# 31 of 135 products of ones taken out of a fused attention and expert layer

## The reference

```
q   = ln(x) * g + b                     # self-attention: 16 heads of width 8
x   = x + mha(q, q)                     # 512 x 512 scores per head
qc  = ln(x) * g + b ;  kv = ln(ctx) * g + b     # ctx: 154 tokens per sequence
x   = x + mha(qc, kv)                   # 512 x 154 scores per head
h   = ln(x) * g + b                     # eight experts, two chosen per token
out = x + sum over the 2 chosen e of gate_e * (gelu(h @ fc1_e.T + b1_e) @ fc2_e.T + b2_e)
```

## Time and profile before

| | |
|---|---|
| median of 3 runs | 272.69 us (272.57 to 273.06) |
| the profiled execution | 272.78 us |
| its span, first to last instruction | 270.8 us |
| TensorE busy | 248.6 us, 1699 matmuls |
| VectorE busy | 184.0 us |
| ScalarE busy | 162.2 us |
| GpSimd busy | 61.6 us |
| mean granted TensorE clock | 0.974 |

### The profile page before, as it was taken

How to read it: one execution, slowest core, us unless ns; L and a number is a source line. 1 busy time by engine, 2 the same in 40 slices (tenths; PEclk the granted TensorE clock), 3 DMA queues, 4 the chain that set the end, 5 groups by cost and what they waited for, 6 DMA issues and landing times.

```text
span 270.8 us, 5195 instructions
## 1 busy us (share of the span) xinstructions
PE 248.6 (92%) x1699; PEld 141.1 (52%) x1699; DVE 184.0 (68%) x369; ACT 162.2 (60%) x289; POOL 61.6 (23%) x110
## 2 busy tenths in 40 slices
PE   6899999999999999899999999998999999999540
PEld 2354533433333433345453455334699999999430
DVE  3859689999989889567554499764377455455543
ACT  3383465676776879869676413871576776766300
POOL 3560000000022020000222020175105700036372
PEclk9999999999999999999999999999999999999955
DMA  7107131240322220530110310013302261122232
GB/s 238 43 9 282 68 90 44 69 113 18 87 65 84 80 80 2 165 114 0 28 61 5 87 32 5 4 50 93 86 19 61 74 189 41 31 59 61 68 87 69
DMA packets 18634, 19.37 MB, mean 72 GB/s; under 512 B 2805, under 2 KB 15025, under 8 KB 18609
## 3 DMA queue, kind: packets, MB, share of 16 engines
q1 hardware_dynamic: 15089, 10.36, 13.2%
q10 hardware_dynamic: 2496, 6.59, 7.6%
q0 software_dynamic: 1024, 2.10, 2.7%
HBM read 9.13 MB, written 5.51 MB: 54 GB/s over the span
## 4 chain that ended last, share of the span: by engine, by line
PE 78%; DVE 9%; issue 3%; POOL 3%; ACT 2%; DMA 2%; POOLq 1%; DVEq 0%; ACTq 0%
PE ps_o L1108 11%; PE ps_r L1184 10%; PE ps_r L1175 10%; PE ps_r L1088 9%; PE ps_o L971 7%; PE ps_r L1046 6%; PE ps_x L946 3%; PE ps_r L982 3%; DVE row_max L808 2%; PE ps_o L1120 2%; PE ps_x L971 2%; PE ps_r L1058 2%; PE ps_o L1115 2%; PE ps_x L975 2%; ACT probs L654 2%
## 5 line engine op out<-in xcount | busy, mean ns | idle before, releaser
L654 ACT ACTIVATE probs<-ps_r 128x1024 f32<-128x1024 f32 (+1 forms) x88 | 83.6, 984 | 26.1 <-PE ps_r L1088 23.2
L804 DVE TENSOR_REDUCE row_max<-ps_r 128x2 f32<-128x1024 f32 x64 | 76.0, 1222 | 13.4 <-PE ps_r L1046 11.9
L704 ACT ACTIVATE parts<-ps_r,staged 128x128 f32<-128x128 f32 x120 | 33.2, 379 | 17.2 <-PE ps_r L1175 16.0
L1108 PE MATMUL ps_o<-probs,v_aug 128*9 128x512 f32 x256 | 33.3, 594 | 0.0
L541 POOL CAST max_part<-row_max 128x16 fp32r<-128x16 f32 x16 | 3.1, 196 | 128.9 <-issue 92.8
L971 PE MATMUL ps_o<-ones_bf 128*128 128x512 bf16 x114 | 32.4, 382 | 0.0
L1175 PE MATMUL ps_r<-rows_T,staged 128*128 128x128 f32 x240 | 30.8, 277 | 0.5 <-DVE staged L893 0.5
L1046 PE MATMUL ps_r<-k_tile,q_tile 32*128 32x512 f32 x128 | 29.9, 480 | 0.9 <-ACT probs L654 0.7
L1184 PE MATMUL ps_r<-staged,parts 128*128 128x128 f32 x240 | 30.7, 275 | 0.0
L1088 PE MATMUL ps_r<-q_tile,k_tile 32*128 32x512 f32 x128 | 29.3, 484 | 1.5 <-ACT probs L654 1.0
L808 DVE TENSOR_REDUCE row_max<-ps_r 128x4 f32<-128x616 f32 x32 | 24.3, 794 | 8.1 <-PE ps_r L1058 7.8
(11 more groups left out here) (161 smaller groups left out, 282.9 us busy)
## 6 DMA issues: line engine op xcount, KB each, us to landing
fc_sb<-fc_w ACTq DMA_DIRECT2D x8, 514.0 KB, 3.6
q_tile<-parts SPq DMA_DIRECT2D x36, 64.0 KB, 2.1
places_in<-o_raw ACTq DMA_DIRECT2D x2, 960.0 KB, 5.2
places_out<-rows_in SPq DMA_DIRECT2D x30, 64.0 KB
rows_in<-places_in SPq DMA_DIRECT2D x6, 256.0 KB, 3.4
k_tile<-parts SPq DMA_DIRECT2D x12, 64.0 KB, 2.1
x_sb<-x SPq DMA_DIRECT2D x2, 256.0 KB, 4.6
fc_sb<-w_rep SPq DMA_DIRECT2D x1, 512.0 KB, 5.3
```

What stands on the lines that cost most here:

```text
L654: nc.scalar.activation(probs[:, i:i + w], ps_r[:, slot("s", r), 0:w], ACT.Exp, scale=SCALE).then_inc(s_read, 1)
L704: ins = nc.scalar.activation(hidden[:, n % HIDDEN, c], ps_r[:, slot("s", r), 0, c * P:c * P + P], ACT.Gelu, bias=staged[:, o % STAGES, 2 * ...
L804: nc.vector.tensor_reduce(heads[:, 2 * pair:2 * pair + 2, t], ps_r[:, slot("m", r)], AX.X, ALU.max).then_inc(m_read, 1)
L1108: mm = nc.tensor.matmul(ps_o[32 * j:32 * j + DH + 1, :], v_aug[:, b, c, 4 * g + j], probs[:, region(n) + j], start=first, stop=last, tile_ ...
```

## The change

Where a word goes away altogether, its wait goes with it. The core of the diff, from the first and the last third of the list:

```
-    ... qk0:2 warm:1 max:1 warm:1 qkl:1 warm:5
-    qkl:2 ctx_hat:0 v:0 max:4 clear:3 zero:0 warm:5 max:3 ...
+    ... qk0:2 warm:1 max:1 qkl:1 warm:2 qkl:2
+    ctx_hat:0 v:0 max:4 clear:3 zero:0 warm:3 max:3 ...
...
-    max:82 neg:12 max:86 proj:2 warm:5 mT:12 ln:4 max:84 max:87
-    max:90 hat:4 warm:3 max:95 neg:13 warm:5 mT:13 max:88 max:91 warm:3 hT:4 max:89 warm:2 max:93 warm:2 router:0
+    max:82 neg:12 max:86 proj:2 warm:3 mT:12 ln:4 max:84 max:87
+    max:90 hat:4 warm:3 max:95 neg:13 warm:4 mT:13 max:88 max:91 warm:2 hT:4 max:89 warm:2 max:93 warm:2 router:0
...
-    oc:15 oT:15 warm:5 osT:3 warm:2 proj:3 warm:3 gT:0 ln:5 hat:5 warm:6 xT:0 warm:3 hT:5 fc1:0
+    oc:15 oT:15 warm:4 osT:3 proj:3 warm:2 gT:0 ln:5 hat:5 warm:1 xT:0 warm:3 hT:5 fc1:0
```

More of the change, by code:

```diff
@@ L69 @@
 ORDER_OF_STEPS = """
[L70 to L89, removed]
@@ L90 @@
-    pv:32 oc:8 scores:75 scores:67 neg:10 ln:3 oT:8 scores:74 hat:3 warm:1 pv:35 mT:10 pv:34 oc:9 hT:3 scores:73
-    warm:1 pv:39 q:3 scores:72 pv:38 oc:11 scores:71 oT:9 scores:70 pv:37 oT:11 pv:36 warm:2 max:80 oc:10 oT:10
-    max:83 max:81 warm:2 max:85 warm:1 osT:2 warm:1 max:82 neg:12 max:86 proj:2 warm:5 mT:12 ln:4 max:84 max:87
-    max:90 hat:4 warm:3 max:95 neg:13 warm:5 mT:13 max:88 max:91 warm:3 hT:4 max:89 warm:2 max:93 warm:2 router:0
-    scores:81 rank:0 scores:79 neg:14 warm:5 mT:14 scores:80 max:92 pv:43 max:94 neg:15 scores:77 prefix:0 scores:76
@@ L95 @@
[L95 to L108, removed]
+    ln:0 hat:0 ln:1 ctx_ln:0 hT:0 hat:1 clear:0-1 warm:4 qk0:0-1 clear:2 qk0:2 warm:1 max:1 qkl:1 warm:2 qkl:2
+    ctx_hat:0 v:0 max:4 clear:3 zero:0 warm:3 max:3 max:0 warm:1 max:5 warm:3 max:7 hT:1 qk0:3 max:2 warm:2 max:6
@@ new lines @@
+    v:1 neg:0 qkl:3 warm:3 mT:0 fill:0 warm:1 max:22 max:17 max:23 k:1 warm:5 scores:6 max:20 warm:1 scores:4 warm:3
+    max:19 warm:3 scores:1 max:21 ctx_T:0 max:16 warm:1 scores:7 warm:1 max:18 warm:3 scores:3 max:28 pv:3 max:24
+    scores:5 neg:2 warm:1 mT:2 max:25 max:31 max:8 q:1 scores:0 pv:2 scores:2 max:11 scores:19 warm:2 max:26 warm:1
+    ctx_vA:0 scores:23 max:30 pv:0 max:29 scores:20 max:27 warm:2 scores:18 max:15 pv:1 oc:0 neg:3 max:12 scores:17
+    mT:3 max:10 warm:1 pv:9 scores:22 load_fc:0 max:13 oT:0 scores:16 scores:21 max:14 pv:11 max:47 scores:30 max:9
@@ new lines @@
+    pv:10 scores:24 max:43 pv:8 max:42 scores:27 warm:2 max:53 neg:1 mT:1 oc:2 scores:31 max:54 ctx_k:0 scores:25
+    warm:2 max:45 scores:26 pv:15 max:49 scores:28 load_fc:1 max:44 pv:12 scores:29 max:48 warm:1 oT:2 scores:12
+    scores:14 max:41 max:46 warm:3 scores:13 max:40 warm:1 pv:13 scores:10 neg:5 max:51 pv:14 oc:3 max:55 kc_diag:0
+    scores:15 mT:5 max:32 warm:3 scores:9 load_fc:2 max:50 pv:6 scores:11 max:52 pv:7 max:36 scores:8 max:37 neg:6
+    pv:5 mT:6 scores:43 max:38 pv:4 oT:3 oc:1 scores:46 load_fc:3 scores:47 max:33 warm:1 oT:1 scores:40 warm:1
@@ new lines @@
+    max:35 scores:42 warm:1 osT:0 max:34 warm:1 scores:41 max:39 pv:21 neg:4 scores:44 load_fc:4 max:63 proj:0
+    scores:48-49 pv:23 ln:2 max:60 scores:45 pv:20 scores:51 hat:2 warm:1 scores:50 max:59 mT:4 pv:22 scores:52
+    max:58 hT:2 max:56 oc:5 max:61 scores:54 q:2 scores:53 pv:24 scores:32 scores:55 pv:25 max:62 scores:33
+    load_fc:5 pv:26 scores:38 max:57 pv:27 scores:34 max:67 max:66 neg:7 oc:6 scores:39 max:64 mT:7 pv:16 scores:35
+    max:68 scores:37 load_fc:6 oT:5 pv:19 scores:36 max:65 warm:1 max:70 pv:17 max:69 scores:58 ctx_vB:0 scores:56
@@ new lines @@
+    max:78 scores:61 pv:18 oT:6 oc:4 neg:8 scores:59 max:71 scores:60 oT:4 scores:57 max:76 pv:29 mT:8 max:79
+    scores:62-63 neg:9 pv:28 mT:9 max:77 max:74 neg:11 pv:30-31 oc:7 mT:11 max:72 scores:66 scores:65 load_fc:7
+    warm:2 oT:7 max:75 scores:64 pv:33 osT:1 max:73 scores:69 scores:68 proj:1 pv:32 oc:8 scores:75 scores:67 neg:10
+    ln:3 oT:8 scores:74 hat:3 warm:1 pv:35 mT:10 pv:34 oc:9 hT:3 scores:73 warm:1 pv:39 q:3 scores:72 pv:38 oc:11
+    scores:71 oT:9 scores:70 pv:37 oT:11 pv:36 warm:2 max:80 oc:10 oT:10 max:83 max:81 warm:2 max:85 warm:1 osT:2
@@ new lines @@
+    warm:1 max:82 neg:12 max:86 proj:2 warm:3 mT:12 ln:4 max:84 max:87 max:90 hat:4 warm:3 max:95 neg:13 warm:4
+    mT:13 max:88 max:91 warm:2 hT:4 max:89 warm:2 max:93 warm:2 router:0 scores:81 rank:0 scores:79 neg:14 warm:5
+    mT:14 scores:80 max:92 pv:43 max:94 neg:15 scores:77 prefix:0 scores:76 scatter:0 words:0 pv:42 oc:13 mT:15
+    scores:78 scatter:1 scores:84 scores:83 pv:40-41 oT:13 gates:0 oc:12 scores:82 stage:0 warm:1 scores:86
+    scatter:2-3 scores:85 pv:45 pv:44 load_rows:0 oc:14 scores:87 stage:1 oT:12 stage:2 pv:46 oT:14 pv:47 stage:3
@@ new lines @@
+    oc:15 oT:15 warm:4 osT:3 proj:3 warm:2 gT:0 ln:5 hat:5 warm:1 xT:0 warm:3 hT:5 fc1:0 router:1 fc1:1-2 rank:1
+    fc2:0 xT:1 fc2:1 save:0 fc1:3 stage:4-5 prefix:1 fc1:4-5 scatter:5 save:1 scatter:4 fc2:2 xT:2 stage:6 fc2:3
+    stage:7 fc2:4 stage:8 fc1:6 scatter:7 save:2 fc2:5 save:3 stage:9 fc1:7 fc2:6 stage:10 fc1:8 fc2:7 stage:11
+    scatter:6 fc1:9-10 save:4 xT:3 fc2:8-9 save:5 fc1:11 stage:12-13 save:6 fc2:10 save:7 fc1:12 stage:14 save:8
+    words:1 load_rows:1 fc2:11 fc1:13 stage:15 fc1:14 fc2:12 xT:4 stage:16 fc2:13 stage:17 fc2:14 fc1:15-17 stage:18
@@ new lines @@
+    fc2:15 stage:19 xT:5 fc2:16 stage:20 fc1:18 fc2:17 fc1:19 stage:21 fc2:18 fc1:20 stage:22 fc1:21 xT:6 fc2:19
+    stage:23 save:9 fc2:20 fc1:22 stage:24 fc2:21 save:10 fc1:23-24 stage:25 save:11 fc2:22 fc1:25 save:12 xT:7
+    save:13 stage:26 save:14-15 fc2:23 stage:27 fc1:26 save:16 fc2:24 stage:28 gather:1 fc1:27 fc2:25 gather:2
+    save:17-18 stage:29 save:19 fc1:28 save:20 fc2:26 fc1:29 save:21-22 fc2:27 save:23 fc2:28 save:24 gather:0
+    gather:3 save:25 fc2:29 save:26-29 b2:0 comb:1 gather:5 comb:2 comb:0 store:2 gather:7 comb:3 gates:1 gT:1
@@ L109 @@
+    gather:4 b2:1 store:3 store:0-1 comb:5 comb:7 comb:4 gather:6 store:7 comb:6 store:5 store:4 store:6
 """
```

## The result

The changed kernel takes 269.6 us (median of 4 runs, 269.41 to 269.70) against 272.66 us before; the ratio is 0.9883, 95% interval 0.9867 to 0.9898. The forecast was 270.4 with a range of 269.3 to 271.9: the direction and the mechanism held, the gain was 3.1 where 2.24 was forecast. The profiled execution took 269.57 us, its span 267.8. Only 2.8 us of the gain lie inside the span, the stretch from the first to the last instruction (median 270.7 before, 267.9 after); the time around it fell as well, from 2.0 us in the executions of the kernel before to 1.7 in those of the kernel after.

A forecast was written before the change was run, and what follows sets the result against it. TensorE looked like the bound (busy 248.6 of 270.8 us), partly with unread ones. Of 31 removed, 16 give nothing and 15 give 2.24 us: 272.69 - 2.24 = 270.4 us, range 269.3 to 271.9.

The forecast's parts named there:

- the last eight: Removed ones at `osT:3`, `proj:3` and `hat:5`: hidden by waits for ACT's oT and DVE's layer norm, worth 0.
- the 1.98 us around the span: Time of the profiled execution outside its 270.8 us span, claimed untouched by the change.
- each further one moves TensorE by 0.216: Price per removed product of ones, from six in a row taking 1.46 us against 0.38 for a single one.
- The bounds by releases: A step can move only to about 0.15 us behind its release: 0.23 at `scores:4`, 0.23 at `max:89`.
- four places of the middle: `max:27`, `max:13`, `max:33`, `scores:60`: steps behind wait for other engines, worth 0; 0.9 us together if not covered.
- the first router: Sign: logits at 167.55 move near 165.6; under 1 us or over 2.6 us would mean the forecast was wrong.
- rival C: Much more of the removed ones is on the path, as chain shares say: 5.9 us, giving 266.8; chance 0.02.
- Rival A: Clock falls once at 188 to 193 us, costing 1.4 us of experts' products: 271.8; chance 0.10.
- my rule that two falls are needed for a slower kernel: At 1.4 us per clock fall, the kernel becomes slower than before from the second fall on (2.8 us).
- B: DVE, nearly full from 31 to 108 us, takes back the opening's gain: 271.1 if half arrives, 271.8 if none; chance 0.12.
- D: The removed ones only turn into waiting everywhere: 272.7; chance 0.04.
- E: Slower: clock falls in three thinned stretches, 15 to 31, 154 to 167, 184 to 193 us: 274.7; chance 0.05.

The follow-up runs named there:

- e9: Kernel before with three products of ones instead of one at `scores:83`, two instead of one at `pv:10`, none instead of two at `hat:2`; 273.13 us, ratio 1.0026.
- e3: Kernel before with only the opening's 11 products of ones removed (`max:1` to `k:1`); 270.85 us, ratio 0.9929.
- e5: Kernel before with one product of ones removed at each of six middle places (`max:27`, `max:13`, `pv:10`, `max:33`, `hat:2`, `scores:60`); 272.11 us, ratio 0.9977.
- e1: Kernel before with only the 16 products of ones removed that the prediction priced at nothing; 272.23 us, ratio 0.9979.
- e7: Kernel before, unchanged, profiled once more; 272.69 us.
- e6: Kernel after without its last ten products of ones (`oT:15`, `proj:3`, `hat:5`, `xT:0`); 271.94 us, ratio 0.9973.
- e4: Kernel before with all 135 products of ones removed, the fourteen ahead of the list kept; 287.45 us, ratio 1.0525.
- e10: Kernel after with its last ten products of ones replaced by transposes; no time given, mean clock 0.972 to 0.976.

## Why the prediction was right, and where its sizes were off

The method, asking at each place what the next real step waited for, held. The terms, as forecast and as the shifts in the trace after give them:

| place | forecast | measured |
|---|---|---|
| landing of the input | 0 | 0.18 |
| `max:1`, `qkl:1` | 0.55 | 0.66 |
| `zero:0` | 0.41 | 0.44 |
| `neg:0`, `qkl:3` | 0.15 | 0.19 |
| `k:1` | 0.23 | 0.23 |
| `pv:10` | 0.14 | 0.30 |
| between `pv:10` and `hat:2` | 0 | 0.06 |
| `hat:2` | 0.216 | 0.20 |
| near 121 us | 0 | 0.17 |
| `proj:2`, `neg:13`, `max:91` | 0.23 | 0.23 |
| `scores:83` | 0.216 | 0.33 |
| `oT:15` | 0.09 | 0.06 |
| the last eight | 0 | 0 |

They sum to 2.23 and 3.05, and the two spans differ by 3.0. Not all of the measured column is owed to the products: the landing is scatter, and near 121 us the kernel before moves by 0.11 by itself.

One term was put at nothing without a reason: the 1.98 us around the span, "which the change does not touch". In the four executions of the kernel after they are 1.70 to 1.77, so a quarter of a microsecond of the gain is none of the places'. That the forecast missed it has little to do with its mechanism; no run tells why it fell.

The step inside the span that was mis-sized is "each further one moves TensorE by 0.216". It is right for a further one and short by 0.10 for the only one of a group. It was measured inside a series of six and used on singles. That accounts for `scores:83` and, with the bound of 0.216 that I laid on it and then halved, for `pv:10`: e9 shows both. `max:1` was a single too, but its place was bound by ACT's rounded key at 16.62 in my sum; the trace after has `qkl:2` at 16.45, that is 16.62 less the 0.18 of the landing, so that bound was met, and the further 0.11 came behind it: the pair of L990 and the projection started closer together. Why they did, no run tells.

The bounds by releases held where I used them: 0.23 at `scores:4` (it now starts at 32.68, 0.14 behind the reductions that end at 32.54), 0.23 at `max:89`, and nothing at the last eight. At `max:89` some of it may not be the product's: the eight products ahead of it take 0.05 less in the kernel after than in the kernel before, and in e3 and e5 0.12 came there for nothing. Calling four places of the middle covered held too (e5).

Of the signs that were to tell, the reductions (18.51, 19.69 and 29.05 for 18.8, 20.0 and 29.4), `scores:4`, the clock and the place behind `hT:5` came as forecast, the times up to 0.8 us earlier. One sign against the forecast was tripped: the first router moved by 2.64 us, over the 2.6 that was to mean rival C. C is not true for that, since it asked for 5.9 us and e1's sixteen products would then have given 3; the mark stood too near the forecast of 1.93 to bear the surplus of `max:1`, `pv:10`, the landing and the step near 121 us.

Rival A did not come true, with four and four executions of the kernel after at 269.41 to 269.96, but there is no one price for a fall. The 1.4 us was read from one execution of the opening, in which the fourteen ones took 4.58 us; they take 6.04 in e7 and 6.00 in the kernel after. The fall of e6 cost 0.7, the long one of e4 nearly 8. So my rule that two falls are needed for a slower kernel leaned on a wrong size: a single one like that at 35 us would have been enough. B is refuted by e3, C by e1, D by the result, and E did not happen, though e4 shows its mechanism.

## What to carry to other kernels

A filler product is on the path only where the next real step starts later than the release it waits for; read that gap at each place, and price the product at no more than the gap. Take the price of one from the same surroundings: alone between real products it was 0.32 here, in a series 0.216. Products that cost nothing where they stand may be just those that hold the clock, so take out the ones that cost, keep the ones that idle would replace, and look at the spread of executions and not at one. Compare the time around the span too: here it held a quarter of a microsecond that no place accounts for.

## What the runs showed of the hardware that was not expected

- The clock stayed at 0.50 for 27 us while TensorE was busy 88% of the time (e4, 35.5 to 62.8), and rose again without idle time; the other falls of that run lasted between 3.4 and 20.5 us.
- Twenty transposes of float32 held the clock at 1.00 as ten products of ones did (e10), where with neither it fell in the profiled execution (e6), and by the mean clock in all twelve.
- The same program, thinned too far, takes 270.2 in one execution and 273.7 in another (e6), with a mean clock of 0.967 and 0.948. The kernel after stays within 0.6 us in its eight executions. The kernel before is not free of such falls: 6 of the 56 executions that stand beside the experiments took 273.95 to 274.79 with a mean clock of 0.968 or 0.969, where the others have 0.971 or more. Eight executions are too few to tell whether the change made them rarer or more frequent.
- One product of ones (128x512, bf16) among products on 32 rows moved what stood behind it by about 0.32 us, each further one by 0.216 (e9).
